# Expert feed-forward chains: GpSimd alternates row scatters and row gathers after the first eight gathers

## The reference

```
# layer 2: 8 experts, layer norm per expert, relu        (once)
assign = argmax(x @ centroids.T)
y      = x + relu(norm(x) @ W1[assign] + b1[assign]) @ W2[assign] + b2[assign]
# layer 3: 16 experts, silu, weight of the top expert     (four times in a row)
probs  = softmax(x @ router_n); w = max(probs); idx = argmax(probs)
x      = w * (silu(x @ W1[idx]) @ W2[idx])                # W1: 128 x 512, W2: 512 x 128
```

## Time and profile before

| | us |
|---|---|
| median of 3 runs (lowest to highest) | 879.82 (878.84 to 885.58) |
| the profiled execution | 878.3 |
| its span, first to last instruction | 876.5 |
| mean granted TensorE clock in it | 0.928 |
| TensorE busy with matmuls | 721.6 (82%) |
| GpSimd busy | 291.4 (33%) |

### The profile page before, as it was taken

One profiled execution on the slowest core, in us unless ns is written; L12 is line 12 of the kernel. 1 busy time (PEld: TensorE's weight loads), 2 busy tenths in 40 slices (PEclk: granted clock), 3 DMA queues, 4 the chain that ended last, 5 costly groups with the idle time before them and its releaser, 6 DMA issues.

```text
span 876.5 us, 15643 instructions
## 1 busy us (share of the span) xinstructions
PE 721.6 (82%) x6143; PEld 433.4 (49%) x6169; DVE 438.7 (50%) x1182; ACT 284.7 (32%) x477; POOL 291.4 (33%) x324
## 2 busy tenths in 40 slices
PE   6799915999997898998787998787967987797774
PEld 3365612774554575655444565344524543453443
DVE  5566487663445775655454555533253334324332
ACT  3233310123332514442153343233314422333332
POOL 7212211222211322322655221343264226433442
PEclk9999966999999879998798999999998899999998
DMA  6900060040000000000215300120111012111212
GB/s 136 328 6 2 26 192 7 19 165 29 1 1 1 0 1 1 1 1 1 58 26 149 83 1 2 43 34 31 40 33 35 22 34 40 34 35 29 34 32 67
DMA packets 43759, 39.03 MB, mean 45 GB/s; under 512 B 11648, under 2 KB 34720, under 8 KB 43560
## 3 DMA queue, kind: packets, MB, share of 16 engines
q1 hardware_dynamic: 37240, 26.88, 10.6%
q0 software_dynamic: 5120, 10.50, 5.4%
q10 hardware_dynamic: 1328, 0.66, 0.3%
HBM read 30.75 MB, written 7.27 MB: 43 GB/s over the span
## 4 chain that ended last, share of the span: by engine, by line
PE 67%; DVE 14%; issue 8%; DMA 4%; another core or an unknown queue 2%; POOL 2%; ACT 2%; DVEq 0%; SPq 0%; POOLq 0%; ACTq 0%
PE psum L1615 9%; PE psum L1638 8%; PE psum L548 8%; PE psum L506 7%; PE psum L1625 5%; PE psum L570 4%; PE psum L495 3%; PE psum L582 2%; PE psum L709 2%; PE psum L1201 2%; PE psum L591 2%; PE psum L1182 2%; DVE scr L929 1%; DVE scr L895 1%
## 5 line engine op out<-in xcount | busy, mean ns | idle before, releaser
L289 POOL TENSOR_TENSOR scr<-KT,hmask 128x512 f32<-128x512 f32 x64 | 67.7, 1064 | 158.0 <-PE psum L548 63.2
L1483 DVE COPY scr<-psum 128x512 f32<-128x512 f32 x64 | 44.3, 692 | 136.0 <-PE psum L1625 88.2
L406 DVE TENSOR_REDUCE Mp<-psum 128x8 f32<-128x1024 f32 x64 | 78.5, 1226 | 63.8 <-PE psum L506 27.5
L313 ACT ACTIVATE scr<-psum 128x1024 f32<-128x1024 f32 x64 | 65.5, 1023 | 120.4 <-PE psum L548 44.7
L463 PE MATMUL psum<-fill,identb 128*128 128x512 bf16 x300 | 78.6, 401 | 1.9 <-issue 1.2
L548 PE MATMUL psum<-Qa,scr 64*128 64x128 f32 x1024 | 73.9, 284 | 0.0
L506 PE MATMUL psum<-scr 64*128 64x512 f32 x256 | 71.8, 638 | 0.0
L548 PEld LDWEIGHTS psum<-Qa,scr 64*128 64x128 f32 x1024 | 63.3, 188 | 15.6 <-issue 10.4
L1625 PEld LDWEIGHTS psum<-ident,scr 128*128 128x128 f32 x304 | 33.9, 148 | 65.1 <-issue 57.1
L1615 PE MATMUL psum<-KT,xsT 128*64 128x512 f32 x120 | 35.7, 668 | 31.2 <-issue 31.2
L1365 POOL DMA_INDIRECT yb_d<-scr,tok x44 | 42.8, 972 | 54.9 <-ACT scr L1313 49.4
(11 more groups left out here) (345 smaller groups left out, 1248.5 us busy)
## 6 DMA issues: line engine op xcount, KB each, us to landing
big<-in_L_ffn_W SPq DMA_DIRECT2D x2, 2048.0 KB, 9.0
big<-in_L_ffn_W SPq DMA_DIRECT2D x8, 512.0 KB, 9.6
big<-in_L_ffn_W SPq DMA_DIRECT2D x1, 4096.0 KB, 13.5
b1r<-in_L_ffn_b SPq DMA_DIRECT2D x1, 2048.0 KB, 10.9
scr<-yb_d SPq DMA_DIRECT2D x6, 256.0 KB, 3.1
xn_d<-xn SPq DMA_DIRECT2D x2, 512.0 KB, 3.2
scr<-ya_d SPq DMA_DIRECT2D x4, 256.0 KB, 3.0
yb_d<-scr,tok POOLq DMA_INDIRECT x44
```

What stands on the lines that cost most here:

```text
L289: pool.tensor_tensor(Km[:, i % 2, c, :, :], KT[:, c, i, :].unsqueeze(1).to_broadcast([P, HV, P]), hmask4[:, :].unsqueeze(2).to_broadcast([ ...
L313: act.activation(PT[i % 2][:, c, :], pair(weights_unit(i, c)), ACT.Exp, scale=SCALE).then_inc(S(f"exp{c}"), 1)
L406: dve.tensor_reduce(Mp[:, HC * c:HC * c + HC, DH:DH + 1], pair(scores_unit(i, c)).rearrange("p (j k) -> p j k", j=HC), AX.X, ALU.max, nega ...
L1483: ins = dve.tensor_copy(hTg[:, g % 2, :], bank[[3, 6][g % 2]])
```

## The change

GpSimd's list in a chain is reordered. It issues the first eight gathers, then (in layer 2) the three additions into `x`, waits for `tok_ready`, and then for each group g in turn issues the scatter of group g, after its `y_ready`, and behind it the gather of group g + 8, if there is one. The waits of each DMA are the ones that it had. No instruction is added or removed on any engine, and the lists of the other engines do not change.

```diff
-            for g, q in enumerate(order(li)):
+
+            def gather(g):
+                q = order(li)[g]
                 if g >= XG:
                     pool.wait_ge(S("xsT_ps"), chain_group(li, g - XG) + 1)
                 pool.indirect_dma_start(xsg[:, g % XG, :], None, from_d[li + 1][0:B * P + P, :],
                                         bass.IndirectOffsetOnAxis(rowi[:, q:q + 1], 0)
                                         ).then_inc(S(f"rows_in{g % XG}"), 16)
+
+            def scatter(g):
+                q = order(li)[g]
+                pool.wait_ge(S("y_ready"), chain_group(li, g) + 1)
+                pool.indirect_dma_start(to_d[li + 1][:, :], bass.IndirectOffsetOnAxis(tok[:, q:q + 1], 0),
+                                        ysg[:, g, :], None).then_inc(S("rows_out"), 16)
+
+            for g in range(XG):
+                gather(g)
             if li < 0:
...
             pool.wait_ge(S("tok_ready"), k.route + 1)
-            for g, q in enumerate(order(li)):
-                pool.wait_ge(S("y_ready"), chain_group(li, g) + 1)
-                pool.indirect_dma_start(to_d[li + 1][:, :], bass.IndirectOffsetOnAxis(tok[:, q:q + 1], 0),
-                                        ysg[:, g, :], None).then_inc(S("rows_out"), 16)
+            for g in range(k.nb):
+                scatter(g)
+                if g + XG < k.nb:
+                    gather(g + XG)
```

## The result

| | before | after |
|---|---|---|
| median of 4 runs each on one chip, us (lowest to highest) | 882.02 (878.84 to 885.58) | 846.79 (843.65 to 847.25) |
| ratio, with its 95% interval | 1 | 0.9608 (0.9569 to 0.9646) |
| the profiled execution, us | 878.3 | 846.73 |
| its span, us | 876.5 | 844.9 |
| mean granted TensorE clock | 0.928 | 0.929 |

The change made the kernel faster by 3.9%. The forecast was 862 us with 832 to 890 as its range; the time lies in it, but under the forecast's own 850 to 873. The mean granted clock of the two profiled executions is the same within 0.001, so the clock is not what changed.

A forecast was written before the change was run, and what follows sets the result against it. TensorE, busy 82% of the span, was taken as the bound, its handovers held up by dense GpSimd DMAs. From 878.3 us, 15 for four layer-3 chains and 2 for layer 2 gave 861, forecast 862 us; range 832 to 890.

The forecast's parts named there:

- The bound and the mechanism: TensorE bounds the kernel, busy 82% of the span; dense GpSimd DMAs hold up its handovers, single ones do not.
- The run of six goes: Layer-3 chains, groups 7 to 9: six back-to-back scatters vanish, which cost 5.2 us, 0.87 us per DMA.
- The eight pairs: Layer 3, groups 2 to 10: scatter plus gather per group adds 0.95 us, giving 3.6 us a group (2.67 to 3.95).
- First run and clock: Layer-3 chains: first run ends after eight gathers, first two groups stay 5.3 us; one slower-clock product charged 0.9 us.
- Layer 2: Layer-2 chain: eight gathers, additions that hold up nobody, then four pairs; half of 4.0 us delay gained, 2 us.
- Gathers in time, end of the chain: Layer 3: later gathers still land with 7 us to spare; last scatter and following load stay put; both cost nothing.
- The pauses stay or move: Layer-3 pauses are not GpSimd's doing, so they stay or only move: 880 us, chance 0.18.
- Pairs free: Layer-3 pairs cost nothing, since only runs of three or more DMAs hurt: 828 us, chance 0.16.
- Standing still for each pair: Layer 3, groups 2 to 10: TensorE's handovers stop during each pair, 5.2 us a group: 913 us, chance 0.17.
- The signs: No six-scatter run or 5 us idle; groups 2-10 even 3.3-3.95 us, waits under 2 us, groups 11-15 at 2.67 us.

The follow-up runs named there:

- scatters in twos: Kernel before, layer-3 piled-up scatters released two per group, gathers unchanged: 827.2 us (0.9995) on the chip without pauses, 855.58 us (0.9746) on one with them.
- the extra runs: Two kernels: changed kernel plus extra GpSimd or SP operations behind group 9's scatter, another kind in each layer-3 chain: 860.49 us and 864.96 us.
- two close variants of its order: Changed kernel with twelve gathers first in layer 3, 828.11 us (1.0016); changed kernel with two scatters then two gathers, 826.25 us (0.9976).
- the second trace of this kernel: Kernel before, unedited, run once with a profile on another chip that has the pauses: 877.82 us.
- the variant with the long first run: Changed kernel with twelve gathers instead of eight ahead of layer 3's first scatter: 828.11 us (1.0016) without pauses, 852.37 us (0.9712) with them.
- gathers later: Kernel before, layer-3 gather g + 8 also waits for group g's output, scatters stay behind all gathers: 838.9 us, 1.0160, chip without pauses.

## Why the prediction was right, and where it was off

**The bound and the mechanism.** Right on the chips that show the pauses: a run of indirect DMAs delays TensorE's handovers (scatters in twos takes the pause away, the extra runs bring it back elsewhere). Too wide in one word: it said dense GpSimd DMAs, and plain ones do nothing. And on one chip the mechanism is absent; the changed kernel itself did not run there, but two close variants of its order did no better than the kernel before.

**The run of six goes**: right. The step to group 9 fell from 7.3 to 7.8 us to 2.7 to 3.2. The price was off in two ways. It stopped at group 9: the next two groups took 4.93 and 3.17 us, 2.8 more than at full pace, so that the run cost 8.0 us in li = 1 and not 5.2 (and with the gather at 667.91, 0.30 us ahead of the first scatter, it is a run of seven). And 0.87 us for each DMA was the wrong unit; that is what misled the next term.

**The eight pairs**: the step that was mis-sized. Taken was 0.95 us for a pair, 3.6 us a group; measured from group 2 to group 10 are 2.92, 3.11, 3.17 and 3.08 us a group in the four chains, 0.40 a pair, below even the half of 0.65. Even that is too much for the pairs: the step from group 2 to group 3, 3.2 to 4.4 us, lies beside the end of the eight gathers, before the first pair. From group 3 to group 12, where the pairs stand, it is 0.30 to 0.41 a pair. The term was built by charging each DMA of a run alike. The measured runs show otherwise: four in a row cost about 1 us together, a run of five 1.8, one of eight 7.4, so the last ones cost most. A run that ends in a wait for a fresh output never gets to the expensive part; when it slows TensorE, its own next scatter comes later.

The trace of before had a short run with its price, and the prediction read it wrongly: three scatters back to back in layer 2 (442.90 to 446.51) "did no harm". Beside and behind them TensorE, and VectorE for the transposes of 445.34:

```profile
444.33 1.08 PE L1615 MATMUL psum<-scr,xsT 128*64 128x512 f32 x4
...
447.24 0.69 DVE L1480 TENSOR_TENSOR scr<-psum,nb 128x512 f32<-128x512 f32 x1 [2.12 <-PE psum L1625]
...
448.18 1.08 PE L1615 MATMUL psum<-big,xsT 128*64 128x512 f32 x4 [1.05 <-DVE xsT L1462]
```

VectorE took transposes that would end at 446.00 only at 447.24, and the group took 3.85 us, 1.2 more than at full pace (3.67 us in the second trace of this kernel). That is 0.4 a DMA, less than half of 0.87.

With 0.40 in the place of 0.95 the prediction's sum for li = 1 gives 5.3 + 8 x 3.07 + 0.9 = 30.8 us, 7.9 less than before, four such 32 us: 878.3 - 32 - 2 = 844 us, against 846.7 for the profiled execution.

**First run and clock**: the first two groups were left at 5.3 us and took 4.7 (636.08 to 640.81); the step behind them is 4.2 us in li = 1, 1.5 us over full pace, for which the sum had no term of its own. The charge of 0.9 us was right in kind, but it came at a chain's start. In li = 2 three products ran at the lower level of the clock:

```profile
708.14 1.98 PE L1626 MATMUL psum<-big,xsT 128*64 128x512 f32 x4 [0.56 <-DVE xsT L1476]
711.00 1.97 PE L1626 MATMUL psum<-KT,xsT 128*64 128x512 f32 x4 [0.48 <-DVE xsT L1476]
715.00 1.97 PE L1626 MATMUL psum<-big,xsT 128*64 128x512 f32 x4 [0.77 <-DVE xsT L1476]
```

That chain gained 4.5 us where the others gained 8.6 to 9.2.

**Layer 2**: forecast 2 us, measured 2.8 from first to last group (35.6 to 32.8). Three pairs ran in a row there, and a new delay of 1.9 us came up beside them, at group 6; the first four groups gained 3.0 us. That the additions "hold up nobody" is not so: they hold VectorE. Its copies of 5 columns (`nbd`) take 0.15 to 0.41 us elsewhere in the chain, and 1.25 us beside an addition in the changed kernel (at 437.59), where TensorE lost nothing by it. In the variant with the long first run on the chip without pauses they take 1.95 and 1.24 us (431.09 and 433.29) and end with the additions beside them; TensorE took 4.44 us for that group and waited 1.64 us of it for VectorE.

**Gathers in time, end of the chain**: both right. TensorE's transposes of li = 1 sat idle once for 0.2 us and never for a gather. From the last W1 product to the last scatter 679.45 to 685.88 is 6.43 us; 697.81 to 704.25 in the earlier trace rows is 6.44.

**The rivals.** The pauses stay or move (880 us): refuted for the chips on which the kernel before takes 878 to 882 us. The statement behind it, in the Trainium skill's "SBUF — State Buffer", section "Who interferes with whom", that a DMA never contends with a compute engine, is what the 826.55 us chip shows and what the twelve plain stores show; the indirect runs on the others speak against the forecast that follows from it, with 7.4 us. The page speaks of ports of SBUF, and no run shows that the delay arises there. Pairs free (828 us): in the price of a pair nearer than the forecast, 0.40 where it had 0 and the forecast 0.95; in time, at 846.8 us, a little farther. Standing still for each pair (913 us): refuted, TensorE is 23.12 of 25.00 us busy.

**The signs.** The run of six and the idle piece of 5 us are gone, as forecast. Two signs came out only in part, both for the reason above: the W1 products do not come at an even 3.3 to 3.95 us but at 2.6 to 3.7 us in turns, with a single 4.2 to 4.4 early in three of the chains (groups at the lower clock not counted), and the longest unexplained waits of VectorE and ScalarE for TensorE are 3.4 and 3.9 us, not under 2. Groups 11 to 15 run at 2.67 us in li = 0 and li = 1; in the other two the steps are up to 0.6 us longer until group 13. That the forecast of 15 us for four chains met 31.0 is no success of the sum: the range of 832 to 890 was wide enough.

## What to carry to other kernels

Space out indirect DMAs of GpSimd: alternate gathers and scatters, and let each wait for something that the busy engine has just handed over, so that a run ends by itself. When a term is priced from a long run, don't divide it by the run's length; look for short runs in the trace and read what each of them costs, until the busy engine is back at full pace. And time such a change on more than one chip: the same kernel took 826.6 us on one and 878 to 881 us on four others, and what spacing is worth on those it was not worth on the one.

## What the runs showed of the hardware that was not expected

- On four of five chips, indirect DMAs issued back to back from GpSimd (1.25 us each) delayed what VectorE and ScalarE got from TensorE: three extra ones by 1.8 us, six by 7.4. Twelve plain DMAs of the same 64 KB from GpSimd, 0.55 us each, in the same queue and in as many packets, delayed nothing, nor did six on SP's queue or six copies on GpSimd.
- On the fifth chip eleven back-to-back scatters left TensorE 14.70 of 14.70 us busy, and sixteen (gathers later, li = 1, 659.73 to 678.87) left it at 2.64 to 2.70 us a group. Why the chips differ, and what in the chip delays the handover (the matmul, its semaphore, or the step between), stays open: the profile names no releaser, only "issue" and "remote".
- Behind the pause at group 9 TensorE's next W1 product took 1.29 to 1.98 us instead of 1.08 in the four chains of the kernel before, and that group 4.1 to 4.9 us instead of 2.67 (granted clock 0.50 from 679.03 to 683.90): a pause costs 1.4 to 2.3 us beyond its own length.
- An addition on GpSimd held a copy of VectorE until it ended: 1.24 to 1.95 us for 5 columns that take 0.15 to 0.41 us otherwise.
